# Layer four's attention: the mask's product over the scores in two halves of eight heads, the addition behind it waiting for the first half only

## The reference, cut to what matters

```python
def attention(q, k, v, mask):
    scores = jnp.einsum('bhqd,bhkd->bhqk', q, k) / jnp.sqrt(jnp.float32(HD))
    scores = scores * mask - 10000.0 * (1.0 - mask)
    probs = jax.nn.softmax(scores, axis=-1)
    return jnp.einsum('bhqk,bhkd->bhqd', probs, v)
...
ctx = merge_heads(attention(split_heads(q), split_heads(k), split_heads(v), ltor_mask))
...
ctx = merge_heads(attention(split_heads(q), split_heads(k), split_heads(v), cross_mask))
```

## Time and profile before

| | us |
|---|---|
| Median of 3 runs | 2345.29 |
| Lowest and highest run | 2340.04 and 2346.04 |
| The profiled execution's own time | 2333.35 |
| Its span, first to last instruction | 2331.6 |
| Mean granted clock of TensorE over the span | 0.949 of full speed |
| Busy: PE, DVE, ACT, POOL | 2082.6 (89%), 944.8 (41%), 995.9 (43%), 658.7 (28%) |
| Layer four's attention, of the span | 1850 to 2200 |

### The profile page before, as it was taken

One profiled execution on the slowest core, in us unless ns is written; L12 is line 12 of the kernel. 1 busy time (PEld: TensorE's weight loads), 2 busy tenths in 40 slices (PEclk: granted clock), 3 DMA queues, 4 the chain that ended last, 5 costly groups with the idle time before them and its releaser, 6 DMA issues.

```text
span 2331.6 us, 37925 instructions
## 1 busy us (share of the span) xinstructions
PE 2082.6 (89%) x15565; PEld 1649.3 (71%) x15565; DVE 944.8 (41%) x1726; ACT 995.9 (43%) x2601; POOL 658.7 (28%) x768
## 2 busy tenths in 40 slices
PE   7877788887899999999899999999889877878799
PEld 4555566654688888888788888888755555666566
DVE  3433222302454444445454444444311267667510
ACT  3332344351343443434343343434344356666522
POOL 2311212112232231313223132321120156656500
PEclk9987899997999999999999999999989898989899
DMA  4000000001010000000001000000020100000000
GB/s 135 10 6 1 6 1 1 1 1 41 3 44 19 10 28 1 28 1 19 1 19 46 1 28 10 10 1 1 1 83 0 46 1 2 6 1 6 1 19 19
DMA packets 28174, 38.36 MB, mean 16 GB/s; under 512 B 1744, under 2 KB 19808, under 8 KB 28000
## 3 DMA queue, kind: packets, MB, share of 16 engines
q1 hardware_dynamic: 28000, 35.93, 4.8%
HBM read 33.83 MB, written 2.10 MB: 15 GB/s over the span
## 4 chain that ended last, share of the span: by engine, by line
PE 75%; DVE 8%; ACT 8%; issue 3%; POOL 3%; DMA 1%; SPq 0%; DVEq 0%; ACTq 0%; POOLq 0%
PE ps L184 33%; PE ps L2105 6%; PE ps_four L2251 5%; PE ps_four L2271 4%; PE ps_four L2089 4%; PE ps L2089 3%; PE ps_four L2260 2%; ACT l_pt L1472 2%; POOL l_sm L1322 2%; PE ps_four L2019 2%; PE ps L2147 2%; DVE l_sm L1829 2%; PE ps L2281 1%; PE ps L2057 1%; PE ps L2065 1%
## 5 line engine op out<-in xcount | busy, mean ns | idle before, releaser
L1566 ACT ACTIVATE l_prob<-ps_four,l_mx 128x129 f32<-128x129 f32 x512 | 181.3, 367 | 593.5 <-DVE l_mx L1864 593.5
L1356 POOL TENSOR_TENSOR l_prob<-l_prob,l_mx 128x516 f32<-128x516 f32 x128 | 134.1, 1048 | 779.5 <-DVE l_mx L1871 779.5
L184 PE MATMUL ps<-l_hT,l_wq 128*128 128x512 f32 x768 | 210.8, 410 | 6.5 <-DVE l_V L1852 6.5
L184 PE MATMUL ps<-ctxT,l_wk 128*128 128x512 f32 x768 | 214.3, 415 | 0.0
L184 PEld LDWEIGHTS ps<-l_wo,l_ao 128*128 128x128 f32 x1536 | 197.8, 188 | 21.1 <-DVE l_ao L1883 7.0
L184 PE MATMUL ps<-l_wo,l_ao 128*128 128x256 f32 x1536 | 204.9, 283 | 5.5 <-DVE l_ao L1883 5.5
L184 PE MATMUL ps<-l_wv,ctxT 128*128 128x512 f32 x768 | 204.6, 402 | 3.7 <-POOL l_wv L1294 3.4
L1322 POOL TENSOR_TENSOR l_sm<-l_sm,l_mask 128x1024 f32<-128x1024 f32 x64 | 149.9, 2363 | 155.7 <-DVE l_sm L1829 155.7
L184 PEld LDWEIGHTS ps<-l_wv,ctxT 128*128 128x128 f32 x768 | 143.8, 190 | 47.4 <-ACT l_qT L1547 9.0
L1795 DVE TENSOR_TENSOR x_tok<-x_tok,ps 128x512 f32<-128x512 f32 x100 | 64.7, 684 | 274.1 <-PE ps L2105 212.1
L184 PEld LDWEIGHTS ps<-l_hT,l_wq 128*128 128x128 f32 x768 | 135.8, 190 | 30.3 <-issue 7.2
(11 more groups left out here) (230 smaller groups left out, 3797.6 us busy)
## 6 DMA issues: line engine op xcount, KB each, us to landing
l_staging<-in_L_xattn_wv SPq DMA_DIRECT2D x8, 512.0 KB, 3.8
l_staging<-in_L_xattn_wk SPq DMA_DIRECT2D x8, 512.0 KB, 3.9
l_staging<-in_L_xattn_wq SPq DMA_DIRECT2D x8, 512.0 KB, 4.2
l_staging<-in_L_xattn_wo SPq DMA_DIRECT2D x8, 512.0 KB, 3.8
x_tok<-in_x SPq DMA_DIRECT2D x4, 512.0 KB, 7.4
ctx_tok<-in_ctx SPq DMA_DIRECT2D x4, 512.0 KB, 5.8
l_mlp_w<-in_L_xattn_mlp_w SPq DMA_DIRECT2D x2, 1024.0 KB, 8.8
l_w<-in_L_xattn_w_fc SPq DMA_DIRECT2D x2, 1024.0 KB, 6.3
```

Of the source, the lines that this page charges most:

```text
L184: ins = e.matmul(out, a, b, start=start and i == 0, stop=stop and i == 2, skip_group_check=not check)
L1356: e.tensor_tensor(pr[:, :, 0:S + 1], pr[:, :, 0:S + 1], mx[:, 3, :].unsqueeze(2).to_broadcast([P, GB, S + 1]), ALU.mult).then_inc(sem("poo ...
L1566: ins = e.activation(pr.t[:, b, 0:S + 1], banks[b // 2].t[:, (b % 2) * (S + 2):(b % 2) * (S + 2) + S + 1], ACT.Exp, bias=mx[:, 1, b:b + 1] ...
```

## The change

VectorE's product becomes two products of eight heads each. The first gives a semaphore of its own, `dve.l3_scores:a`; the second frees the PSUM group, as the whole product did. GpSimd's first addition waits for the new semaphore, its second one for the freeing of the group.

```diff
@@ gpsimd_program, l3_scores
-            q.wait_ge(*pl.event(("empty", "four", "l3", n, 0)))
             for i, name in enumerate(("pool.l3_scores:a", "pool.l3_scores")):
+                if i == 0:
+                    q.wait_ge(*pl.done("dve.l3_scores:a", n))
+                else:
+                    q.wait_ge(*pl.event(("empty", "four", "l3", n, 0)))
                 half = sm[:, 8 * i:8 * i + 8, :]
                 e.tensor_tensor(half, half, mask.unsqueeze(1).to_broadcast([P, 8, S]), ALU.add).then_inc(sem(name), 1)
@@ vector_program, l3_scores
-            e.tensor_tensor(sm.t[:], bk.t[:].rearrange("p r (x t) -> p (r x) t", t=S),
-                            mask.unsqueeze(1).to_broadcast([P, 16, S]), ALU.mult).then_inc(bk.slot.empty, 1)
+            for i in range(2):
+                heads = bk.t[:, 2 * i:2 * i + 2, :].rearrange("p r (x t) -> p (r x) t", t=S)
+                e.tensor_tensor(sm.t[:, 8 * i:8 * i + 8, :], heads, mask.unsqueeze(1).to_broadcast([P, 8, S]), ALU.mult).then_inc(
+                    sem("dve.l3_scores:a") if i == 0 else bk.slot.empty, 1)
```

## The result

| | before | changed |
|---|---|---|
| Median of 4 runs, us | 2342.66 | 2319.41 |
| Lowest and highest run, us | 2337.08 and 2346.04 | 2313.54 and 2321.14 |
| Profiled execution, us | 2333.35 | 2321.14 |
| Ratio of changed to before, with 95% interval | | 0.9906 (0.9881 to 0.9931) |

The change is faster by 23 us by the medians, 16 to 28 by the interval. The direction and the stage were right, the size was not. The forecast counted from the median of three runs of before, 2345.3; the median of four is 2342.7. So of the 12.1 us between 2331.5 and 2319.4, 2.6 come from where the forecast started and 9.5 from the size of the gain.

A forecast was written before the change was run, and what follows sets the result against it. A handshake between VectorE, GpSimd and TensorE in layer four's attention, no engine's work alone, was taken as the bound; 10.6 + 3.2 = 13.8 us off 2345.3 gave 2331.5 us, range 2323 to 2342.

The forecast's parts named there:

- VectorE's wait: VectorE's wait for GpSimd's addition in layer four's attention: down from 50.2 to about 25 us.
- TensorE's share of the stage: TensorE's busy share of layer four's attention, from 1850 us on: up from 0.77 to about 0.80.
- the counted units: Units (one batch row's 16 heads each) 0, 1, 4, 5, 6, 10, 14, 15, 18, 19, 21, 25, 28, 30, 31: 13.8 us together.
- the other 17: The attention units of 32 said to gain nothing; the account was that TensorE is late there.
- B: Rival: TensorE takes over as its gaps in the attention fill up; gain 6.8 us or less, 2338.5 to 2345; 22%.
- C: Rival: GpSimd's addition holds up VectorE's second half product; 13 us slower, 2358; 4%.
- E: Rival: GpSimd's first wait still ends with the second half; time as before; no chance of its own beside B.
- 10.6 + 3.2 = 13.8: Gain in us over layer four's attention: ten units at the whole 1.06, plus five units gaining part of it.
- D: Rival: shorter waits keep TensorE's clock up, 11 us on top, 2320, or cost 3 to 5; 6% for more than A, 9 to 18.
- the ten full units: Attention units 1, 4, 5, 6, 10, 14, 18, 25, 28, 31: the whole 1.06 us each, 10.6 us.
- five partial units: Attention units 21 (0.67 us), 0 (about 0.7), 30 (0.84), 15 and 19 (about 0.5 each): 3.2 us together.
- unit 5: A full unit, 1.06 us, gaining by GpSimd: both additions, L1335, then TensorE's L2078, which stood 4.32 us for it.

The follow-up runs named there:

- before's two: The kernel before, unchanged: its first profile and a second one from timing it against itself, ratio 1.0000 (0.9982 to 1.0018).
- changed, again: The changed kernel, unchanged, timed against the kernel before and profiled a second time: ratio 0.9899 (0.9872 to 0.9927).
- changed, delayed: The changed kernel with one VectorE memset ahead of the attention's first product, timed against the kernel before: ratio 0.9924 (0.9908 to 0.9939).
- both delayed ones: The kernel before and the changed kernel, each with one VectorE memset ahead of the first product; against the kernel before: ratios 1.0006 and 0.9924.
- the quarters: Against the kernel before: product and additions split into 4, 4 and 8 heads, first reduction into two of 4; ratio 0.9885, median 2313.5 us.

## Why the prediction was wrong, point by point

**Right.** The bound (the handshake, not an engine's work), the price of a half product (1216 forecast, 1215 measured), the second half unhindered beside GpSimd, 0.08 us for the second instruction, VectorE's wait (25 and 22.9), rounds of 8.2 us, TensorE's share of the stage (0.80), and the counted units as a group: alone they give all the gain, the other 17 alone nothing. B is out by that, C by the products' durations, E by GpSimd's start.

**The step that failed: the sum "10.6 + 3.2 = 13.8", what a counted unit is worth, with "nothing" for all other units and next to nothing for D, the clock.** The gain by place, in us: the first row is nine of the ten full units (the tenth, unit 31, has its round behind the stage), from the rounds of the profiles, against the mean of before's two.

| | forecast | changed | changed, again | changed, delayed |
|---|---|---|---|---|
| nine full units | 9.5 | 8.6 | 9.5 | 9.4 |
| five partial units | 3.2 | 4.6 | 4.6 | 4.7 |
| the 17 others | 0 | 1.1 | 4.6 | 2.9 |
| behind the stage (unit 31 and on) | 1.1 | 3.3 | 1.5 | 1.4 |
| together | 13.8 | 17.6 | 20.2 | 18.4 |

That the full units come out within 1 us is luck: unit 5 gave 1.6 to 2.6 us too much, and units 1, 18 and 25 gave 0.15, 0.32 and 0.15 us where each had 1.06, together 2.6 too little (1.7 in the delayed run, where unit 1 gave its 1.06).

*The partial units were mis-sized.* I took VectorE's idle time before the first reduction as the most that a round can gain: 0.67 us for unit 21, 0.7 for unit 0. Both rounds became 1.06 to 1.08 us shorter. What the round waits for last is not the first reduction but GpSimd's *second* addition: in 27 of the 32 rounds before and in 27 and 26 of the changed kernel's, the shift (two inputs in SBUF) ends 1.08 or 1.09 us after that addition does, however early the shift began; in the others it begins after the addition has ended. Unit 21's shift and its two additions, before and changed:

```profile
2089.03 2.10 DVE L1839 TENSOR_TENSOR l_sm<-l_sm,l_mx 128x1024 f32<-128x1024 f32 x1
...
2085.37 4.68 POOL L1322 TENSOR_TENSOR l_sm<-l_sm,l_mask 128x1024 f32<-128x1024 f32 x2 [8.35 <-DVE l_sm L1829]
```

```profile
2082.45 1.85 DVE L1844 TENSOR_TENSOR l_sm<-l_sm,l_mx 128x1024 f32<-128x1024 f32 x1
...
2078.54 4.68 POOL L1325 TENSOR_TENSOR l_sm<-l_sm,l_mask 128x1024 f32<-128x1024 f32 x2 [8.06 <-DVE l_sm L1834]
```

The shift ends 2091.13 - 2090.05 = 1.08 us after the additions before, and 2084.30 - 2083.22 = 1.08 now, though it took 2.10 us and now takes 1.85. A late first reduction only makes the shift's stretch shorter. Both additions start some 1.06 us earlier, so the whole 1.06 comes through. Units 15, 19 and 30 gave 0.7 to 1.0 for 0.5, 0.5 and 0.84. Together some 1.4 us more than the account's 3.2.

*Unit 5 was worth 2.7 us and, in the second profile, 3.7, not 1.06.* Its round on GpSimd and TensorE (and the shift on VectorE), of the kernel before, of the changed one, and of the changed one again:

```profile
1908.57 1.71 POOL L1335 TENSOR_TENSOR l_ao<-l_ao,l_den 128x256 f32<-128x256 f32 x1
...
1910.33 5.35 PE L2078 MATMUL ps<-l_w_ao,l_ao 128*128 128x256 f32 x16 [4.32 <-POOL l_ao L1335]
```

```profile
1909.42 1.70 POOL L1338 TENSOR_TENSOR l_ao<-l_ao,l_den 128x256 f32<-128x256 f32 x1
...
1911.18 3.72 PE L2083 MATMUL ps<-l_w_ao,l_ao 128*128 128x256 f32 x16 [2.15 <-POOL l_ao L1338]
...
1909.23 1.31 DVE L1844 TENSOR_TENSOR l_sm<-l_sm,l_mx 128x1024 f32<-128x1024 f32 x1
```

```profile
1898.30 0.73 POOL L1338 TENSOR_TENSOR l_ao<-l_ao,l_den 128x256 f32<-128x256 f32 x1
...
1899.08 3.72 PE L2083 MATMUL ps<-l_w_ao,l_ao 128*128 128x256 f32 x16 [0.18 <-POOL l_ao L1338]
...
1899.11 1.23 DVE L1844 TENSOR_TENSOR l_sm<-l_sm,l_mx 128x1024 f32<-128x1024 f32 x1
```

The division (L1335, now L1338) ends 5.94 + 1.70 = 7.64 us after the product's start, where it ended at 6.98 + 1.71 = 8.69: 1.05 us, as forecast. But the output product behind it then takes 3.72 us in place of 5.35: the mean granted clock over it is 1.00 of full speed where it was 0.69, after 2.15 us of idle time and not 4.32. That is 1.6 us more. And in the second profile the division takes 0.73 us and not 1.70, since it is over before VectorE's shift begins (L1844 at 1899.11, 0.08 after its end). That is 1 us more again. In the changed kernel's first profile the shift had begun 0.19 us before the division. It is so throughout: in these three profiles the division takes 0.72 to 0.74 us where no shift is running when it starts, and 1.05 to 1.74 where one is.

*The clock gave more than it took.* Rival D had 6%. TensorE's busy time in the stage, for the same 3312 recorded matmuls, for before and for the two profiles of the changed kernel:

```profile
1850.66:2187.98 337.32, 262.69 (x3312) 204.74 (x3312) 238.97 (x234) 214.80 (x548) 211.07 (x103) 0.90 0.03 11
```

```profile
1856.14:2179.07 322.93, 259.06 (x3312) 202.58 (x3312) 239.52 (x265) 215.20 (x548) 209.09 (x103) 0.91 0.04 11
```

```profile
1845.49:2163.97 318.48, 257.36 (x3312) 200.83 (x3312) 239.43 (x265) 214.21 (x548) 209.41 (x103) 0.91 0.04 11
```

It is 262.7 us before (263.1 again, 265.2 delayed), 259.1 and 257.4 after (254.1 delayed): 3.6 us less or more, for the same matmuls. How much of that was on the path cannot be read off. It is not all one way: the clock gave unit 5 its 1.6 us and took 1.8 from units 1 and 25, and at the start of unit 23's round, 2.05 us longer, 32 matmuls of the values take 1.94 us where they took 1.08. Behind the stage, 2.2 and 0.4 us beyond unit 31's 1.06 went with it.

**What adds up, and what doesn't.** The profiles show 17.6, 20.2 and 18.4 us; the ratios of the same three runs give 22, 24 and 18, with intervals from 16 to 28, 17 to 30 and 14 to 22. These agree within the noise, and the forecast of 13.8 lies below all three intervals; but where the 4 us are that the first two ratios have more is open. One part may be this: the layers before the attention, whose code is the same (582.7 to 1676.0 us in the profile of before), took 3.1 and 3.3 us less in the two profiles of the changed kernel than in the first of before. The second of before took the same as the first; all other runs but the quarters (3.1 less), both delayed ones among them, took 1.1 to 1.5 us less. That was not tested and may be chance. The wait for the bias row's DMA, 20.1 to 26.1 us over all profiles, adds up to 6 us to an execution of any of the kernels, and is part of why runs of one kernel lie up to 19 us apart.

**The range** failed with the sum: its lower end, 2323, was 18 us for every pass of the chain, some clock and 3 us of spread, counted from a median that was itself 2.6 us high. The time lies 3.6 us below that end; 2.6 of these come from that median, which is chance. One reading of the account was loose besides: it is L1365 that waits 6.18 us in unit 24, and the addition behind it starts 3.38 us after the product, 1.0 later than usual. Unit 24 gave nothing all the same.

## What to carry to other kernels

Before costing an earlier start, follow the round to what ends it last: here not the operation that waited for the first half, but the one held by the second addition, so idle time before the first was the wrong measure. A unit-by-unit walk along the chain found the group of units that carries the gain, though not how it is shared among them; switching the edit on for chosen units is a cheap test of it. On a TensorE that idles in bursts each saved microsecond also moved where its clock falls, so the range should have several us for that on either side. Measure a stage in two or three profiles before a difference of a few us is explained.

## What the runs showed of the hardware

- VectorE's product with one input in PSUM takes no longer beside GpSimd's addition in SBUF (1191 to 1225 ns over 64), while VectorE's operation with both inputs in SBUF takes 2.12 us beside it and 1.23 alone, and ends 1.08 us after the addition however early it began. For GpSimd it is the same the other way round: its 256-element product takes 0.73 us with no such operation running when it starts and mostly 1.70 with one.
- Delaying a stage by one memset changed single rounds by 1.65 us in either direction and the stage by 1.8 us. In the round that was followed, TensorE's mean granted clock went from 0.90 to 1.00 and its busy time fell by the same 1.6 us.
- A second instruction in place of one costs VectorE 0.08 us when it follows at once.
